# Three chains cut into halves of 256 tokens, other first loads, and new job orders in a two-layer attention and FFN kernel

## The reference, cut to what matters

```
x = x + xattn(layernorm(x), ctx, Wq, bq, Wkv, bkv, Wo, bo)      # 16 heads, 77 keys
x = x + ffn0(layernorm(x))      # gate/up 352 wide, silu(gate)*up, down; activations
                                # rounded to integers with ONE scale for the whole tensor
x = x + xattn(layernorm(x), ctx, mask, Wq, Wk, Wv, Wo)
x = x + moe(layernorm(x))       # 8 experts of 256, all computed, summed, times a gate
```

## Time and profile before

| | |
|---|---|
| median of 3 runs | 331.54 us (330.99 to 332.46) |
| the profiled execution | 334.84 us, its span 332.7 us |
| TensorE matmul busy | 282.6 us (85%) |
| VectorE busy | 242.4 us (73%) |
| ScalarE busy | 167.6 us (50%) |
| GpSimd busy | 132.7 us (40%) |
| mean granted TensorE clock | 0.927 |

### The profile page before, as it was taken

The page is one execution under the profiler, slowest core; times in us unless marked ns, Lnnn a source line. Parts: engine busy times, 40 slices in busy tenths (PEclk is TensorE's granted clock), DMA queues, the critical chain, the costliest instruction groups (busy, mean ns, idle before and its releaser), DMA issues.

```text
span 332.7 us, 4623 instructions
## 1 busy us (share of the span) xinstructions
PE 282.6 (85%) x1341; PEld 176.5 (53%) x1350; DVE 242.4 (73%) x671; ACT 167.6 (50%) x275; POOL 132.7 (40%) x144
## 2 busy tenths in 40 slices
PE   7977799899877272668899798989999999999994
PEld 3544435445545120234554455445787788888883
DVE  4877269967524789868577688725987999889883
ACT  1510366555783275493236556578444444544541
POOL 5799348321341498013329010314385604305200
PEclk9996799989999658599679999999999999999999
DMA  7675162200007800403223130000000000000000
GB/s 148 161 212 134 37 160 42 75 8 3 8 0 144 217 1 1 127 0 91 55 61 87 26 80 10 1 8 2 0 2 1 0 32 2 2 32 2 0 32 32
DMA packets 12298, 16.91 MB, mean 51 GB/s; under 512 B 3673, under 2 KB 6713, under 8 KB 12266
## 3 DMA queue, kind: packets, MB, share of 16 engines
q1 hardware_dynamic: 9634, 11.23, 13.6%
q0 software_dynamic: 1856, 4.27, 5.3%
q10 hardware_dynamic: 784, 1.14, 1.5%
HBM read 4.90 MB, written 1.05 MB: 18 GB/s over the span
## 4 chain that ended last, share of the span: by engine, by line
PE 47%; DVE 24%; POOL 9%; issue 7%; ACT 6%; SPq 3%; DMA 2%; DVEq 0%; POOLq 0%; ACTq 0%
PE ps_tok L1025 6%; PE ps_key L1034 5%; DVE mx L722 4%; POOL xn L362 4%; PE ps_acc L1161 3%; PE ps_acc L1162 3%; PE ps_acc L1163 3%; PE ps_acc L1189 3%; SPq L300 3%; POOL rstd L358 3%; PE ps_m L1044 2%; DVE stats L630 2%; DVE xn L643 2%; POOL lq L441 2%; ACT big L484 2%
## 5 line engine op out<-in xcount | busy, mean ns | idle before, releaser
L722 DVE TENSOR_REDUCE mx<-ps_tok 128x4 f32<-128x312 f32 x128 | 57.4, 477 | 26.4 <-PE ps_tok L1025 24.6
L484 ACT ACTIVATE big<-ps_key 117x512 f32<-117x512 f32 (+1 forms) x96 | 53.3, 595 | 33.2 <-PE ps_key L1034 32.4
L358 POOL TENSOR_TENSOR rstd<-veps,mhalf 128x4 f32<-128x4 f32 x16 | 16.8, 1049 | 115.3 <-DVE veps L635 115.2
L1025 PE MATMUL ps_tok<-kst,qst 97*128 97x312 f32 x128 | 48.7, 409 | 8.7 <-DVE mx L722 5.6
L870 DVE TENSOR_TENSOR qst<-big,qst 128x512 fp32r<-128x512 f32 x64 | 44.6, 697 | 2.2
L1034 PE MATMUL ps_key<-qst,kst 105*117 105x512 f32 (+1 forms) x96 | 40.8, 450 | 5.2 <-ACT big L484 3.1
L1025 PEld LDWEIGHTS ps_tok<-kst,qst 97*128 97x128 f32 x128 | 25.4, 202 | 33.0 <-DVE mx L722 17.2
L362 POOL TENSOR_SCALAR xn<-x,mv,rstd 128x128 f32<-128x128 f32 x40 | 33.2, 841 | 1.8 <-POOL rstd L358 1.8
L576 ACT ACTIVATE big<-ps_tok,b 128x512 f32<-128x512 f32 x32 | 22.1, 690 | 22.9 <-PE ps_tok L1150 22.0
L576 ACT ACTIVATE big<-ps_key,b 128x512 f32<-128x512 f32 x32 | 22.1, 691 | 22.6 <-PE ps_key L1150 21.5
L947 PE MATMUL ps_key<-spin 128*128 128x512 bf16 x104 | 30.5, 435 | 2.0 <-DVE spin L907 1.4
(11 more groups left out here) (203 smaller groups left out, 533.9 us busy)
## 6 DMA issues: line engine op xcount, KB each, us to landing
qst<-qhi SPq DMA_DIRECT2D x56, 64.0 KB, 2.0
qst<-qlo SPq DMA_DIRECT2D x32, 64.0 KB, 2.0
w1f<-in_w POOLq DMA_DIRECT2D x2, 1024.0 KB, 8.4
kst<-rbuf SPq DMA_DIRECT2D x12, 156.0 KB, 3.7
kst<-rbuf POOLq DMA_DIRECT2D x12, 117.0 KB, 3.1
x<-in_x SPq DMA_DIRECT2D x4, 256.0 KB, 9.3
out<-xn SPq DMA_DIRECT2D x4, 256.0 KB, 2.0
qst<-qhi ACTq DMA_DIRECT2D x8, 64.0 KB, 2.4
```

The lines of the kernel that those rows point to most:

```text
L484: act.activation(p[0:w, j, :], key[n % 2][0:w, :], ACT.Exp, scale=SCALE).then_inc(q["p_ready"], 1)
L722: nc.vector.tensor_reduce(mx[:, u % 2, t, g, 0, :], tok[n % 2][:, 0:KG].rearrange("p (h j) -> p h j", h=HG), AX.X, ALU.max).then_inc(q["to ...
L1025: mm(tok[n % 2][:, 0:KG], qst[0:MASKROW + 1, s, g, 128 * t:128 * t + 128], kst[0:MASKROW + 1, b, g, :], start=True, stop=True).then_inc(q[ ...
```

## The change

**Halves.** Three chains are worked on in halves of 256 tokens, the second half in another PSUM bank, so that a reader of the first half and a writer of the second are never in one bank: LayerNorm, `xt` and `q` of `b == 0` in both layers (second bank `tok[1]`); `ot` and `wo` of the last unit of layer 0 (second bank `acc[0]`), with the statistics of the first two tiles taken before the second half is added; `down` and `dt` of `b == 0` (second bank `tok[1]`). Each gets semaphores of its own.

**First loads.** SyncE loads x(2) and x(3) ahead of the last three quarters of `wqo`. GpSimd runs `rstd_of(0)` ahead of the two loads of `krows` and `ones`.

**Orders.** The lists of ScalarE, VectorE and TensorE are new in both layers, and so are the numbers of spins.

```
-        SPIN = ((8, 1, 8, 3, 5, 5, 0, 1), (2, 2, 1, 2, 0, 0, 11, 6, 1, 6))
-        IDLE = ((7, 6, 1, 4), (10, 0, 0, 5))
+        SPIN = ((12, 1, 18, 5, 0, 0, 1, 2), (1, 3, 1, 2, 3, 1, 1, 9, 5, 7))
+        IDLE = ((7, 0, 0, 4), (11, 0, 0, 1))
...
 SyncE:
             x_load(1)
-            sp.dma_start(wqo[:, 1:4, :], ...)
             x_load(2)
             x_load(3)
+            sp.dma_start(wqo[:, 1:4, :], ...)
...
 GpSimd:
+            rstd_of(0)
             pool.dma_start(kst[96:KROWS, ...], a["krows"]...)
             pool.dma_start(qst[96:97, ...], a["ones"]...)
-            rstd_of(0)
```

The halves, on TensorE, ScalarE and VectorE:

```
 xt on TensorE:
+                            if b == 0 and t == 2:
+                                ins.then_inc(q["xt_half"], 1)
+                                pe.wait_ge(xn_ready[b], 2 * L + 1)
+                            bank = tok[1] if b == 0 and t >= 2 else m0
+                            ins = nc.tensor.transpose(bank[...], xn[:, NT * b + t, :], ident[:, :])
 q on TensorE:
+                            mm(m1[:, 0:256], wq[:, L, :], xt[:, 0, 0:256], ...).then_inc(q["q_half"], 1)
+                            pe.wait_ge(q["xt_copied"], u + 1)
+                            mm(tok[1][:, 256:512], wq[:, L, :], xt[:, 0, 256:512], ...).then_inc(q["q_put"], 1)
 ot on ScalarE, last unit of layer 0:
+                            act.activation(ot[:, 0:256], m0[:, 0:256], ACT.Copy).then_inc(q["ot_half"], 1)
+                            act.activation(ot[:, 256:512], m0[:, 256:512], ACT.Copy).then_inc(q["ot_copied"], 1)
 wo on VectorE, last unit of layer 0:
+                            nc.vector.tensor_tensor(lo, m1[:, 0:256]..., lo, ALU.add).then_inc(q["xa_half"], 1)
+                            dve.wait_ge(q["xa_half"], 1)
+                            ln_stats_of(b, range(2))
+                            dve.wait_ge(q["att_put"], u + 1)
+                            nc.vector.tensor_tensor(hi, acc[0][:, 256:512]..., hi, ALU.add).then_inc(q["x_attended"], 1)
+                            dve.wait_ge(q["x_attended"], u + 1)
+                            ln_stats(B + b, range(2, NT))
 down on ScalarE, b == 0:
+                            act.wait_ge(q["d_half"], 1)
+                            act.activation(dtmp[:, 0, 0:256], acc[0][:, 0:256], ACT.Copy, scale=sdq[:, 0:1])...
+                            act.wait_ge(q["d_put"], 1)
+                            act.activation(dtmp[:, 0, 256:512], tok[1][:, 256:512], ACT.Copy, scale=sdq[:, 0:1])...
```

More of the change, by code:

```diff
@@ L625, in link, with ln_stats_of, ln_stats @@
                 dve.wait_ge(q["dve_self"], link_n[0])
-            def ln_stats(n):
+            def ln_stats_of(b, tiles):
+                for t in tiles:
+                    ins = nc.vector.bn_stats(stats[:, b, t, :], x[:, NT * b + t, :])
+                return ins
+            def ln_stats(n, tiles=range(NT)):
                 b = n % B
-                for t in range(NT):
-                    ins = nc.vector.bn_stats(stats[:, b, t, :], x[:, NT * b + t, :])
-                link(ins)
+                link(ln_stats_of(b, tiles))
                 for t in range(NT):
@@ L644, in ln_apply @@
                                                   rstd[:, b, t:t + 1], ALU.subtract, ALU.mult)
+                    if n in (0, 2 * B) and t == 1:
+                        ins.then_inc(q["xn_half"], 1)
                 ins.then_inc(xn_ready[b], 1)
@@ L724, in attention @@
                     if job == "q":
-                        dve.wait_ge(q["q_hi"], u + 1)
+                        if b > 0:
+                            dve.wait_ge(q["q_hi"], u + 1)
                         if u >= 2:
@@ L728, in attention @@
                                 dve.wait_ge(stack_q[u % 2][g], STQ * (u // 2))
+                        if b == 0:
+                            dve.wait_ge(q["qh_half"], L + 1)
+                            nc.vector.scalar_tensor_tensor(qlo[:, 0, 0:256], m1[:, 0:256], bq[:, L:L + 1], qhi[:, 0, 0:256].bitcast(F32),
+                                                           ALU.add, ALU.subtract)
+                            dve.wait_ge(q["q_hi"], u + 1)
+                            nc.vector.scalar_tensor_tensor(qlo[:, 0, 256:512], tok[1][:, 256:512], bq[:, L:L + 1], qhi[:, 0, 256:512].bitcast(F32),
+                                                           ALU.add, ALU.subtract).then_inc(q["q_lo"], 1)
+                            continue
                         nc.vector.scalar_tensor_tensor(qlo[:, u % 2, :], m1[:, :], bq[:, L:L + 1], qhi[:, u % 2, :].bitcast(F32),
@@ L788, in attention @@
                     if job == "down":
+                        if b == 0:
+                            dve.wait_ge(q["dT_half"], 1)
+                            nc.vector.tensor_tensor(x[:, 0:2, :], acc[0][:, 0:256].rearrange("p (t d) -> p t d", t=2), x[:, 0:2, :], ALU.add).then_inc(q["xf_half"], 1)
+                            dve.wait_ge(q["xf_half"], 1)
+                            ln_stats_of(0, range(2))
+                            dve.wait_ge(q["dT_put"], 1)
+                            nc.vector.tensor_tensor(x[:, 2:4, :], tok[1][:, 256:512].rearrange("p (t d) -> p t d", t=2), x[:, 2:4, :], ALU.add).then_inc(q["x_ffn"], 1)
+                            dve.wait_ge(q["x_ffn"], 1)
+                            ln_stats(2 * B, range(2, NT))
+                            continue
                         dve.wait_ge(q["dT_put"], b + 1)
@@ L993, in down @@
                 for n, tt in halves(b):
+                    bank = tok[1] if b == 0 and n == 2 else acc[b % 2]
                     pe.wait_ge(q["hq_ready"], n)
@@ L996, in down @@
                         w = IT[i3]
-                        ins = mm(acc[b % 2][:, tt], wdT[0:w, i3, :], hq[0:w, b, i3, tt], start=(i3 == 0), stop=(i3 == 2))
-                ins.then_inc(q["d_put"], 1)
+                        ins = mm(bank[:, tt], wdT[0:w, i3, :], hq[0:w, b, i3, tt], start=(i3 == 0), stop=(i3 == 2))
+                    if b == 0 and n == 1:
+                        ins.then_inc(q["d_half"], 1)
+                    else:
+                        ins.then_inc(q["d_put"], 1)
             def attention(L):
@@ L1038, in attention @@
                     if job == "q":
+                        if b == 0:
+                            pe.wait_ge(q["xc_half"], L + 1)
+                            pe.wait_ge(q["wq_in"], 16)
+                            if u == B:
+                                pe.wait_ge(q["wqo_in"], 16)
+                            m1_free()
+                            mm(m1[:, 0:256], wq[:, L, :], xt[:, 0, 0:256], start=True, stop=True).then_inc(q["q_half"], 1)
+                            pe.wait_ge(q["xt_copied"], u + 1)
+                            mm(tok[1][:, 256:512], wq[:, L, :], xt[:, 0, 256:512], start=True, stop=True).then_inc(q["q_put"], 1)
+                            n_q[0] += 1
+                            continue
                         pe.wait_ge(q["xt_copied"], u + 1)
                         pe.wait_ge(q["wq_in"], 16)
-                        if u == B:
-                            pe.wait_ge(q["wqo_in"], 16)
                         m1_free()
@@ L1066, in attention @@
                         for t in range(NT):
-                            ins = mm(m1[:, 128 * t:128 * t + 128], ot[:, 128 * t:128 * t + 128], wo[:, L, :], start=True, stop=True)
+                            if u == B - 1 and t == 2:
+                                ins.then_inc(q["att_half"], 1)
+                                pe.wait_ge(q["ot_copied"], u + 1)
+                            bank = acc[0] if u == B - 1 and t >= 2 else m1
+                            ins = mm(bank[:, 128 * t:128 * t + 128], ot[:, 128 * t:128 * t + 128], wo[:, L, :], start=True, stop=True)
                         ins.then_inc(q["att_put"], 1)
@@ L1094, in attention @@
                     if job == "dt":
-                        pe.wait_ge(q["d_scaled"], b + 1)
+                        if b == 0:
+                            pe.wait_ge(q["ds_half"], 1)
+                        else:
+                            pe.wait_ge(q["d_scaled"], b + 1)
                         for t in range(NT):
-                            ins = nc.tensor.transpose(acc[b % 2][:, 128 * t:128 * t + 128], dtmp[:, b % 2, 128 * t:128 * t + 128], ident[:, :])
+                            if b == 0 and t == 2:
+                                ins.then_inc(q["dT_half"], 1)
+                                pe.wait_ge(q["d_scaled"], 1)
+                            bank = tok[1] if b == 0 and t >= 2 else acc[b % 2]
+                            ins = nc.tensor.transpose(bank[:, 128 * t:128 * t + 128], dtmp[:, b % 2, 128 * t:128 * t + 128], ident[:, :])
                         ins.then_inc(q["dT_put"], 1)
```

61 lines of the change are left out of this document (47 added, 14 removed), and 63 rows, old and new, of the table ORDER.

## The result

In the first comparison, twelve executions of each kernel on one chip, the changed kernel took 330.28 us in the median (328.35 to 334.58) and the kernel before 331.78 (329.63 to 334.31): a ratio of 0.9937, 95% interval 0.9910 to 0.9964, some 2 us. Run once more beside other kernels it gave 330.59 against 331.95, 0.9927 (0.9892 to 0.9961). I had forecast 329.6. By the half per cent that I had set as what can be told, the ratio is just "faster", the outcome I gave 0.46; the two medians alone would be just short of it.

A forecast was written before the change was run, and what follows sets the result against it. Before about 230 us, hand-ordered handoffs between two engines bound it; the experts after are TensorE's own work. Terms -0.5 - 0.5 + 0.6 - 0.85 - 0.7 = -1.95 gave a 329.6 us median, range 326.0 to 333.4.

The forecast's parts named there:

- End of layer 0, -0.5: Copy of ot to the variance: halving lets the first add come 0.73 earlier, less 0.19 on VectorE; 0.5 us gained.
- FFN into layer 1, -0.5: down/0 to q_lo of layer 1: halves bring the first add and q_hi forward; 0.5 us gained (0.2 to 0.9).
- Opening, +0.6: Layer 0 start to key/0/0: later q_lo and q/1 outweigh the gain in xn; net loss 0.6 us (-0.5 to +1.8).
- For q_lo sets the end: Opening: q_lo, not q_hi, ends last; statistics ahead of q/0 put it at 16.6 us instead of 15.5.
- The move takes 2.75: Opening: the move of q_lo takes 2.75 us, so first token scores come at 19.4 us instead of 18.32.
- The 0.7 that I took back in the twelve moves: Opening: q/1's twelve moves on SyncE, starting later, lose less beside GpSimd's key stack; 0.7 us returned.
- Idle matmuls of layer 1, -0.85: At 218.30 us, four of five idle matmuls removed; key/3/0 stood behind them alone, so 0.85 us gained.
- Idle matmuls of layer 0, 0: Seven removed, five of the six at 50.89 us; max/1's move holds key/1/0 anyway: 0 (bound -1.3).
- Orders and clock, -0.7: Layer 1, 157.6 to 164.4 us: five spins behind tok/0/0 may hold the clock; 0.7 us gained (0 to 2.5).
- Rival B: Opening: krows and ones issues starve under VectorE's block, key stack 1.8 to 2.7 us later; 330.3 to 331.1 us; chance 0.25.
- C: Layer 0, near 50.9 us: fewer idle matmuls let the clock fall, up to 1.7 us per stretch; slower, chance 0.15.
- D: Both half-rate stretches after 157 us go and max/1 lands early: 326.6 us; chance 0.15.

The follow-up runs named there:

- e1: The kernel before with the three halved chains alone; orders, idle matmuls and first loads as before: 333.29 us, ratio 1.0027.
- e11: The changed kernel with layer 1's job orders and idle matmuls as before, layer 0's and the halves new: 331.99 us, ratio 0.9991.
- e5: The changed kernel with the statistics of unit 3 behind q/0 again in VectorE's layer 0 list: 330.18 us, ratio 0.9968.
- e12: The kernel before with five idle matmuls put behind tok/0/0 of layer 1: 331.28 us, ratio 0.9997.
- e4: The changed kernel without the five idle matmuls behind tok/0/0 of layer 1: 332.09 us, ratio 1.0014 to the kernel before.
- e2: The changed kernel without the halves, every chain whole; new orders, spins and first loads kept: 331.76 us, ratio 0.9996.
- e10: The changed kernel with layer 0's job orders and idle matmuls as before, layer 1's and the halves new: 331.06 us, ratio 0.9972.
- e6: The kernel before with GpSimd's power of unit 0 moved ahead of the krows and ones loads: 331.66 us, ratio 0.9976.
- e8: The kernel before with one idle matmul instead of five ahead of key/3/0 of layer 1: 332.53 us, ratio 1.0000.

## Why the prediction came out where it did

The time was forecast within 0.7 us. Two terms held, that of the clock about held, the opening had the right sign and a mis-sized move, and one was nothing. That the sum came so close is partly luck: the +0.6 of the opening does not show in the total, and the -0.85 of the idle matmuls was nothing, so two errors nearly offset each other.

- **End of layer 0, -0.5: right.** -0.40 in all eight profiles with halves (3.75 or 3.76 against 4.15 or 4.16). VectorE's extra 0.19 came out exactly (2.41 us from the first add instead of 2.22); the first add came 0.59 earlier and not 0.73.
- **FFN into layer 1, -0.5: right in size, incomplete in cause.** -0.50. I had q_hi coming forward by more than the wait of 0.29, and VectorE free to use it. e1 and e11 show that it isn't: with the old list the same halves give 0.05. The step "leads up to q/0" passed over what that list itself waited for.
- **Opening, +0.6: sign right, hidden in the pair of profiles.** q_lo at 16.44 (16.6 forecast), scores at 18.73 (19.4), SyncE at 24.35 (25.0), key/0/0 at 35.66 (36.9). "For q_lo sets the end" held as to which wait ends last. What failed is "The move takes 2.75": at that time it took 2.23, and e5 shows that q_lo earlier by 1.0 would have bought only 0.13. The 0.7 that I took back in the twelve moves is their scatter between executions. Whether the 0.6 to 1.1 us at key/0/0 reach the end is open (below).
- **Idle matmuls of layer 1, -0.85: wrong, 0.** "key/3/0 stood behind the spins alone; what follows is mostly TensorE's" is the step that failed. key/3/0 did come earlier; on/2, two jobs on, waits for a split on two other engines, and that chain sets the end.
- **Idle matmuls of layer 0, 0**: key/1/0 ran at 51.26, 2.09 after the issue of max/1 at 49.17, so the move holds it, as said. They were not put back alone in the changed kernel, so that term has no measurement of its own.
- **Orders and clock, -0.7: right for the five idle matmuls** (-0.6 by e12; e4 lost 1.4 of mean time), too small for the whole. The clock as a whole gave 0.0052 x 153 = 0.80 us of the 1.69 between the means (332.11 and 330.42); that is an estimate by the slope. What a half-rate stretch costs I had as "up to 1.7"; the slope makes the 3.4-us stretch, 1.7 / 330 = 0.0052 of mean clock, worth 0.8 on average; single ones at 162 to 165 cost 0 to 0.5. The fall that I priced at 1.7 was followed by a second at 168.0, which I had not read, and the two together cost 2.6 in that execution.
- **A reading of the earlier trace rows**: TensorE's row stands at eight or nine tenths from slice 24 on (191 us), not only from 233 us, and the last slice reads 4. No term rests on it.

Rival B fell: the two issues were through at 8.05 (7.51 + 0.54), and krows landed after 5.9 us (before 8.1). The Trainium skill, SBUF — State Buffer, section "SBUF: two separate sides", has GpSimd's descriptors wait while VectorE holds the shared ports. No such wait shows here: the two issues took 0.79 and 0.54 us beside VectorE's xn and copy, and 0.77 and 0.54 in the kernel before, at 1.29 and 2.07, with VectorE idle from 1.38 on. The same section's lock between the two engines' copies agrees with xn at 1.27 instead of 1.82. C fell by the times, though its place is real: two of the seven profiles with layer 0 in its new order fell to half rate at 44.4, none of the others; it cost nothing that can be told (72.26 us from key/0/0 to the power of unit 7 in e5, 72.19 after). D happened in the first profile as to the clock. max/1 was issued there 0.92 earlier than in the first profile of before, but in four other profiles of the old order it was issued at 47.6 to 48.1, earlier than the 49.17 of after: it is the clock of the execution, not the order.

The Trainium skill, TensorE: Matmul & The Clock Gate, section "HAM oscillation — how this bites in real kernels", counts half of the throttled time as lost. Here that is the ceiling: the stretch from q_lo to max/0 of layer 1 has 9.1 us at half rate in the profile of before, so 4.5 could be lost, and it is 2.8 longer than after; over all executions it is 0.153 of 0.33 us for each 0.001 of mean clock, a bit under half of it.

**What stays open.** The halves' 0.4 and 0.5 and the clock's 0.8 make 1.7, which is the difference between the means; so the opening's loss should not reach the end. Each of these numbers is good to a few tenths only. At equal clock that fits the changed kernel (0.88 faster, standard error 0.18), e2 and e12 (no halves in use, 0.15 and 0.04) and e10 (old opening, no faster than the new). It fits e1 and e11 less well, which should gain 0.46 (0.40 from layer 0 and the little of layer 1) and show 0.02 and 0.11, each good to 0.25. It does not fit e6, which has no term of the sum and shows 0.73. By the profiles the start of xn of unit 0 to the power of unit 7, the halves taken out, is 0.2 longer in the mean of seven with the new orders of layer 0 than in that of seven with the old, but 0.8 in the median, and either group spreads over 2.6 us and more. Where the 0.6 to 1.1 us at key/0/0 are given back, if they are, was not found.

## What to carry to other kernels

Before an idle or dummy instruction is priced as time on the path, follow the next shared buffer behind it, not the next instruction: here it was a PSUM bank two jobs on. A chain cut in halves gives only what the next engine's list can take up, so halves and the order of the engine that receives them must be changed together. And where the clock falls in some executions and not in others, profile each kernel twice: of the 5.7 us between the first two profiles, 1.7 were the change. A start-to-landing time read at one moment is not a constant either: the one move priced here at 2.75 us took 2.1 to 3.1.

## What the runs showed of the hardware

The same instruction stream had its twelve queue moves in 8.93 and in 10.46 us, with no difference in the program ahead of them. A move of q_lo issued 1.0 us earlier (e5) took 3.09 us to land instead of 2.23. A window with TensorE busy for 1.77 of 3.0 us was followed by a fall of the clock in one execution (before) and by none in another (e8): with idle matmuls in that place none of seven profiles fell there, without them three of seven did, and the mean clock was 0.9449 against 0.9408. What the falls cost in one and the same part of the kernel ran from nothing (3.4 us at half rate) to 4.3 us (17 us, e1).
